# The second attention with its value steps in pairs, eight exponential slots and no staging copies

## The chip, the core and the metric

The kernel runs a four-layer transformer forward pass as one program on one core of a Trainium2 chip. The metric is the device time of one execution in microseconds. Three executions of the kernel before took 3405.69, 3411.26 and 3417.11 us (median 3411.26).

The engines are named as the profile names them: PE is TensorE (matrix multiply; PEld its weight loads), DVE is VectorE, ACT is ScalarE, POOL is GpSimd, SP is SyncE, which here issues DMAs.

## The reference

The input x has 2048 tokens of 128 features. Each layer adds attention(layernorm(x)) and then ffn(layernorm(x)). The change touches only the attention of layer 1, which reads, cut to what matters:

```python
q = jnp.einsum('bsd,dhk->bshk', x, Wq) + bq      # 16 heads of 64
k = jnp.einsum('bsd,dhk->bshk', x, Wk) + bk
v = jnp.einsum('bsd,dhk->bshk', x, Wv) + bv
q = q / jnp.sqrt(jnp.asarray(depth, q.dtype))     # depth = 64
attn = jnp.einsum('bqhd,bkhd->bhqk', q, k)
attn = jax.nn.softmax(attn, axis=-1)
out = jnp.einsum('bhqk,bkhd->bqhd', attn, v)
return jnp.einsum('bqhd,hdm->bqm', out, Wo) + bo
```

The kernel treats the 2048 rows as one sequence: every head forms 2048 x 2048 scores, takes their softmax over the keys, and multiplies by v.

## The kernel before, in words

The program is a row of stages, two per layer. Stage `l1_attention` (lines 639 to 1011) holds the whole change. It works head by head. A head has 16 key tiles of 128 keys, and its queries are four chunks of 512. A **step** is half a key tile: step n = 2 x (key tile) + (half of the queries), so a head has 32 steps, and one counter g = 32 x head + n runs over all 512 steps. Each engine walks the same counter, in an order that is written out by hand (`tasks_of`, and the loops at the ends of the engines' blocks).

In one step PE does this, in this order:
- `scores(2g)`: one score tile of 128 keys x 512 queries in PSUM (`l1a_st`, three banks). It is two matmuls, L830 (high parts, and low part of q against high part of k) and L832 (the rest, and the row maximum as a 65th row). A bank is free again when ACT has read it;
- the first half of the step's list of **aux tasks**, `tasks[:some]`;
- `scores(2g + 1)`;
- in odd steps `values((g - 3) // 2)`: the value product of one key tile, four matmuls L845 that add into `l1a_ov`, each 64 columns wide, two of them side by side in the array;
- the other half of the aux tasks.

ACT turns every score tile into exponentials (L923), in a ring of `PT_SLOTS` = 6 slots, one slot for a step. DVE adds the exponentials of the even steps into `l1a_acc` (`add_rows`, L995), POOL those of the odd steps (L891). A slot is free when its value product and its sum are done.

Aux tasks share a ring of three PSUM banks (`l1a_aux`). PE writes a bank, DVE reads it, and PE may write the bank of aux task k only when DVE has read that of task k - 3. All in one order. The kinds:
- `max`: one 128 x 512 tile of the scores of the **next** head, with queries in rows (PE L795), and its row maximum (DVE L940). There are 64 in a head, spread over steps 0 to 29 (`MAX_STEPS` = 30). After the last DVE makes the negated maxima (L943);
- `mt`, in step 30: PE transposes them (L798), DVE copies them out (L948), and SP places them by DMA as a row of `l1a_QB` (L760). PE waits at L798 for L943, and all that stands behind it on PE waits too;
- `v`, in steps 15 and 17: the value projection of the next head, eight tiles each, 64 columns of output (PE L803, DVE L961);
- `qk`, in steps 16, 18, 20 and 22: the projection to q and k of the head after the next (PE L800). DVE adds the bias, scales q and writes `l1a_full` (L954). When all four are there, in step 24, ACT rounds it to `l1a_hi` (L903), and POOL, behind its sum of step 27, takes `l1a_lo` = full - hi (`cut`, L878). SP copies hi and lo into the operands `QA`, `KA`, `QB`, `KB`;
- `sum`, `sumT`, `out`, in steps 3, 5 and 7, 9, 11, 13: of the head before, the sums over the keys (L808, copied to `l1a_sums`), their transpose and reciprocal, and the output projection (PE L817), which DVE scales and adds to X (L981).

Before the loop stand, in `before`, the projections of heads 0 and 1, the values of head 0, and all 64 maxima of head 0.

## Time and profile before

| what | value |
|---|---|
| median of three executions | 3411.26 us |
| the profiled execution's own time | 3410.64 us |
| its span | 3408.8 us |
| its mean granted TensorE clock | 0.889 |
| PE busy | 3054.8 us, 90% |
| DVE busy | 2357.4 us, 69% |
| ACT busy | 1438.4 us, 42% |
| POOL busy | 800.2 us, 23% |

The stage runs from about 975 to 2562 us of the span. A busy PE counts each matmul from its start to a modelled end, so matmuls in a row overlap, and how fast PE works is read from the starts of successive rows, not from the busy time. Idle time of PE is real idle time. "PEclk" is the clock that was granted to PE, as a share of 2.4 GHz; it has two levels, 1.0 (2.4 GHz) and 0.5 (1.2 GHz).

### The profile page before, as it was taken

The numbers are of one execution on the slowest core, as the hardware profiler recorded it, in microseconds if no ns is written. First come the engines' busy times: TensorE is split into PE (matmuls) and PEld (weight loads), VectorE is DVE, ScalarE is ACT, GpSimd is POOL, SyncE is SP. The second block draws the span as 40 slices with busy tenths as digits, with TensorE's granted clock in tenths as the row PEclk, the third lists the DMA queues.
The fourth block names the chain that finished last, engine by engine and source line by source line (L and its number), as shares of the span: only waits on it lengthen the run. The fifth ranks groups of instructions, "written<-read, shape, count | busy, mean of one in ns | idle before, by whom it ended". The sixth has DMA issues, their size and how long they took to land. (4 is left out here: it accounts for less than half of the span.)

```text
span 3408.8 us, 44140 instructions
## 1 busy us (share of the span) xinstructions
PE 3054.8 (90%) x16200; PEld 1881.8 (55%) x16200; DVE 2357.4 (69%) x4755; ACT 1438.4 (42%) x2539; POOL 800.2 (23%) x621
## 2 busy tenths in 40 slices
PE   5999999999879999999999999999997574666799
PEld 3766666666545555555555555555543242444576
DVE  5788888888247777777777777777735767665553
ACT  3666666666413444444434444444442203001343
POOL 0000000000012444444434444444340000443100
PEclk7999999999778999999999999999998585555798
DMA  3121121110040111111101111111000000000100
GB/s 89 25 47 31 41 48 42 30 43 1 8 112 1 38 38 38 38 38 25 32 19 38 38 38 38 38 25 36 15 1 12 6 2 1 1 1 3 29 1 13
DMA packets 40395, 95.29 MB, mean 28 GB/s; under 512 B 12262, under 2 KB 29340, under 8 KB 30620
## 3 DMA queue, kind: packets, MB, share of 16 engines
q1 hardware_dynamic: 40180, 92.48, 12.2%
q8 instruction: 128, 2.10, 0.3%
q14 instruction: 87, 0.71, 0.1%
HBM read 34.52 MB, written 7.34 MB: 12 GB/s over the span
## 5 line engine op out<-in xcount | busy, mean ns | idle before, releaser
L923 ACT ACTIVATE l1a_PT<-l1a_st 128x512 f32<-128x512 f32 x1024 | 605.7, 598 | 878.5 <-PE l1a_st L832 871.5
L940 DVE TENSOR_REDUCE l1a_m<-l1a_aux 128x1 f32<-128x512 f32 x1024 | 673.4, 686 | 189.2 <-PE l1a_aux L795 173.8
L441 DVE TENSOR_REDUCE l0s_mquad<-l0s_mx 128x1 f32<-128x512 f32 x1024 | 635.5, 684 | 169.5 <-PE l0s_mx L309 169.5
L891 POOL TENSOR_TENSOR l1a_acc<-l1a_acc,l1a_PT 128x1024 f32<-128x1024 f32 x224 | 555.1, 2478 | 717.2 <-ACT l1a_PT L923 717.2
L417 ACT ACTIVATE l0s_PT<-l0s_st 128x512 f32<-128x512 f32 x1024 | 528.7, 602 | 236.8 <-PE l0s_st L325 234.2
L845 PE MATMUL l1a_ov<-l1a_PT,l1a_V 128*64 128x512 f32 x2048 | 512.3, 622 | 0.0
L830 PE MATMUL l1a_st<-l1a_QA,l1a_KA 128*128 128x512 f32 x1024 | 452.1, 442 | 3.2 <-issue 3.1
L325 PE MATMUL l0s_st<-l_QS,l_KS 128*128 128x512 f32 x1024 | 438.1, 431 | 3.7 <-ACT l0s_PT L417 3.6
L309 PE MATMUL l0s_mx<-l_KS,l_QS 120*128 120x512 f32 x1024 | 415.6, 413 | 20.3 <-DMA l_KS<-qk_rows 20.3
L832 PE MATMUL l1a_st<-l1a_QB,l1a_KB 65*128 65x512 f32 x1024 | 414.7, 405 | 0.0
L795 PE MATMUL l1a_aux<-l1a_KA,l1a_QA 128*128 128x512 f32 x1024 | 404.2, 437 | 6.8 <-DMA l1a_QA<-l1a_lo 5.4
L995 DVE TENSOR_TENSOR l1a_acc<-l1a_acc,l1a_PT 128x1024 f32<-128x1024 f32 x224 | 316.9, 1415 | 68.1 <-ACT l1a_PT L923 55.8
L309 PEld LDWEIGHTS l0s_mx<-l_KS,l_QS 120*128 120x128 f32 x1024 | 328.5, 321 | 64.0 <-DMA l_KS<-qk_rows 21.5
L795 PEld LDWEIGHTS l1a_aux<-l1a_KA,l1a_QA 128*128 128x128 f32 x1024 | 200.9, 196 | 177.8 <-DVE l1a_m L940 113.6
L339 PE MATMUL l0s_ov<-l0s_PT,l_V 128*32 128x256 f32 x4096 | 274.1, 385 | 0.0
L845 PEld LDWEIGHTS l1a_ov<-l1a_PT,l1a_V 128*64 128x64 f32 x2048 | 127.7, 140 | 252.5 <-issue 196.1
L325 PEld LDWEIGHTS l0s_st<-l_QS,l_KS 128*128 128x128 f32 x1024 | 195.3, 192 | 114.9 <-ACT l0s_PT L417 87.0
L830 PEld LDWEIGHTS l1a_st<-l1a_QA,l1a_KA 128*128 128x128 f32 x1024 | 197.6, 193 | 97.4 <-issue 54.5
L871 POOL MEMSET l1a_KB<- 1x4096 f32 x1 | 3.5, 3505 | 948.7 <-POOLq L148 948.7
L832 PEld LDWEIGHTS l1a_st<-l1a_QB,l1a_KB 65*128 65x128 f32 x1024 | 197.7, 193 | 50.0 <-issue 13.5
L339 PEld LDWEIGHTS l0s_ov<-l0s_PT,l_V 128*32 128x32 f32 x4096 | 106.8, 109 | 103.7 <-issue 52.4
L981 DVE SCALAR_TENSOR_TENSOR top_X<-l1a_aux,l1a_rinv,top_X 128x128 f32<-128x128 f32 x256 | 72.0, 344 | 52.6 <-PE l1a_aux L817 51.9
(351 smaller groups left out, 3068.6 us busy)
## 6 DMA issues: line engine op xcount, KB each, us to landing
l1a_KA<-l1a_hi SPq DMA_DIRECT2D x32, 512.0 KB, 8.0
l_QS<-qk_rows SPq DMA_DIRECT2D x64, 192.0 KB
l_KS<-qk_rows SPq DMA_DIRECT2D x64, 192.0 KB
l1a_QA<-l1a_hi SPq DMA_DIRECT2D x16, 512.0 KB, 4.6
...
```

The source lines that it names most:

```text
L309: last = nc.tensor.matmul(o, q[:, tile, :], KS[r, h % BUF0, c * CW:(c + 1) * CW], start=True, stop=True)
L325: nc.tensor.matmul(st[:, b % ST0, :], KS[:, h % BUF0, kt * P:(kt + 1) * P], QS[:, h % BUF0, q:q + CW], start=True, stop=True).then_inc(st_ ...
L339: last = nc.tensor.matmul(ov[32 * q:32 * (q + 1), u % 2, :], V[:, u // 2, 2 * n + e, :], PT[:, (2 * r + e) % PT0, q // 2, at], start=(n == ...
L417: nc.scalar.activation(PT[:, g % PT0, b % 2, :], st[:, b % ST0, :], ACT.Exp).then_inc(exp_done, 1)
L441: nc.vector.tensor_reduce(mquad[:, u % 2, tile, g:g + 1], mx[:, n % MX0, :], axis=AX.X, op=ALU.max).then_inc(mx_free[n % MX0], 1)
L795: last = nc.tensor.matmul(o, QA[:, h % 3, q * P:(q + 1) * P], KA[:, h % 3, c * CW:(c + 1) * CW], start=True, stop=True)
L830: nc.tensor.matmul(st[:, u % ST1, :], KA[:, h % 3, kt * P:(kt + 1) * P], QA[:, h % 3, qc * CW:(qc + 1) * CW], start=True, stop=False)
L832: last = nc.tensor.matmul(st[:, u % ST1, :], KB[:, h % 2, kt * P:(kt + 1) * P], QB[:, h % 2, qc * CW:(qc + 1) * CW], start=False, stop=True)
L845: last = nc.tensor.matmul(ov[HD1 * (qc % 2):HD1 * (qc % 2) + HD1, qc // 2, :], V[:, h % 2, kt, :], PT[:, g % PT_SLOTS, (qc % 2) * CW:(qc % ...
L891: nc.gpsimd.tensor_tensor(acc[:, h % 2, 1, :], first, PT[:, g % PT_SLOTS, :], ALU.add).then_inc(added_pool, 1)
L923: nc.scalar.activation(PT[:, g % PT_SLOTS, (u % 2) * CW:(u % 2 + 1) * CW], st[:, u % ST1, :], ACT.Exp).then_inc(exp_done, 1)
L940: nc.vector.tensor_reduce(m4[:, b, q, c:c + 1], src, axis=AX.X, op=ALU.max).then_inc(aux_read, 1)
```

## The change

It touches eight things of the stage:
- `PT_SLOTS` is 8 instead of 6, and values run in every fourth step: in steps 1, 5, 9, ... PE does the value products of two key tiles one behind the other (`g % 4 == 1`). Key tiles 14 and 15 of a head fall into step 1 of the next.
- `MAX_STEPS` is 28 instead of 30, so the 64 maxima are spread over steps 0 to 27, and `mt` stands in step 29.
- The value projection is done for two heads at once, 128 columns of output: one `v` task of four tiles in steps 15 and 17 of every head but the last two (28 instead of 30 tasks in the loop, 8 PE instructions in each instead of 16).
- `full` is gone. ACT makes each quarter of `hi` from PSUM (Identity with bias, L893), in the step of the `qk` task and behind that step's exponentials. DVE then makes that quarter of `lo` from the same bank (scalar_tensor_tensor, L945), and only then is the bank free. POOL's `cut` is gone.
- q is no longer scaled there; the scale stands in the exponential.
- `sums` is gone (it goes into `acc`), and `osb` has one buffer instead of two.
- DVE no longer waits for its own writes before it frees a bank, and the four output rows of a task have one semaphore update.
- Before the loop, `v` has four tasks, and the `lo` of head 1 stands on DVE ahead of all maxima of head 0.

```diff
-PT_SLOTS = 6
+PT_SLOTS = 8
-MAX_STEPS = 30
+MAX_STEPS = 28
...
-                if n == MAX_STEPS:
+                if n == MAX_STEPS + 1:
                     out.append(("mt", h + 1, 0))
-                if n in (15, 17):
-                    out.append(("v", h + 1, (n - 15) // 2))
+                if n in (15, 17) and h + 2 < H1 + h % 2:
+                    out.append(("v", h // 2 + 1, 2 * (h % 2) + (n - 15) // 2))
...
                     elif kind == "v":
-                        for t in range(8):
-                            last = nc.tensor.matmul(o[:, t * HD1:(t + 1) * HD1], xnT[:, (8 * i + t) * P:(8 * i + t + 1) * P],
-                                                    Wv[:, h, :], start=True, stop=True)
+                        for j in range(TPC):
+                            t = TPC * i + j
+                            last = nc.tensor.matmul(o[:, j * P:(j + 1) * P], xnT[:, t * P:(t + 1) * P],
+                                                    Wv[:, 2 * h:2 * h + 2, :], start=True, stop=True)
...
-                    if g % 2 and 3 <= g < H1 * STEPS1 + 3:
-                        values((g - 3) // 2)
+                    if g % 4 == 1 and 5 <= g < H1 * STEPS1 + 5:
+                        values((g - 5) // 2)
+                        values((g - 5) // 2 + 1)
...
-                def cut(h):
-                    pool.wait_ge(hi_done, h + 1)
...
-                    nc.gpsimd.tensor_tensor(lo[:, :], full[:, :], hi[:, :].bitcast(F32), ALU.subtract).then_inc(lo_done, 1)
...
-                        if kt == 13 and h + 2 < H1:
-                            cut(h + 2)
...
-                def round_hi(h):
-                    act.wait_ge(filled, NC * (h + 1))
-                    if h >= 1:
+                def round_hi(h, i):
+                    act.wait_ge(aux_full, slot[("qk", h, i)] + 1)
+                    if h >= 1 and i == 0:
                         act.wait_ge(placed_a[(h - 1) % 3], 64 * ((h - 1) // 3 + 1))
                         act.wait_ge(placed_b[(h - 1) % 2], 32 * ((h - 1) // 2 + 1))
-                    nc.scalar.activation(hi[:, :], full[:, :], ACT.Copy).then_inc(hi_done, 1)
+                    nc.scalar.activation(hi[:, i * CW:(i + 1) * CW], bank(("qk", h, i)), ACT.Identity,
+                                         bias=bias[:, h:h + 1]).then_inc(hi_done, 1)
...
-                    if n == 24 and h + 2 < H1:
-                        round_hi(h + 2)
+                    if n in (16, 18, 20, 22) and h + 2 < H1:
+                        round_hi(h + 2, (n - 16) // 2)
...
                     elif kind == "qk":
-                        if i == 0 and h >= 1:
-                            dve.wait_ge(lo_done, h)
-                        nc.vector.tensor_scalar(full[:, i * CW:(i + 1) * CW], src, bias[:, h:h + 1], factor[:, :],
-                                                ALU.add, ALU.mult).then_inc(filled, 1)
-                        dve.wait_ge(filled, NC * h + i + 1)
-                        dve.sem_inc(aux_read, 1)
+                        at = slice(i * CW, (i + 1) * CW)
+                        dve.wait_ge(hi_done, NC * h + i + 1)
+                        nc.vector.scalar_tensor_tensor(lo[:, at], src, bias[:, h:h + 1], hi[:, at].bitcast(F32),
+                                                       op0=ALU.add, op1=ALU.subtract).then_inc(aux_read, 1)
```

How the orders stand, at three places. First PE from the last two maxima of step 29 in head 5, in the kernel before, to its step 31:

```order
L795 MATMUL l1a_aux<-l1a_KA,l1a_QA 128x512 x2
L830 MATMUL l1a_st<-l1a_QA,l1a_KA 128x512
L832 MATMUL l1a_st<-l1a_QB,l1a_KB 128x512
L845 MATMUL l1a_ov<-l1a_PT,l1a_V 64x512 x4
L795 MATMUL l1a_aux<-l1a_KA,l1a_QA 128x512
L830 MATMUL l1a_st<-l1a_QA,l1a_KA 128x512
L832 MATMUL l1a_st<-l1a_QB,l1a_KB 128x512
L798 MATMUL l1a_aux<-top_ident,l1a_mneg 16x128
L830 MATMUL l1a_st<-l1a_QA,l1a_KA 128x512
L832 MATMUL l1a_st<-l1a_QB,l1a_KB 128x512
L830 MATMUL l1a_st<-l1a_QA,l1a_KA 128x512
L832 MATMUL l1a_st<-l1a_QB,l1a_KB 128x512
```

The maxima (L795) end with the one behind the value block; two matmuls later stands the transpose L798. After the change, on PE, from the second half of step 27 to step 29 of the same head:

```order
L793 MATMUL l1a_aux<-l1a_KA,l1a_QA 128x512
L829 MATMUL l1a_st<-l1a_QA,l1a_KA 128x512
L831 MATMUL l1a_st<-l1a_QB,l1a_KB 128x512
L829 MATMUL l1a_st<-l1a_QA,l1a_KA 128x512
L831 MATMUL l1a_st<-l1a_QB,l1a_KB 128x512
L829 MATMUL l1a_st<-l1a_QA,l1a_KA 128x512
L831 MATMUL l1a_st<-l1a_QB,l1a_KB 128x512
L796 MATMUL l1a_aux<-top_ident,l1a_mneg 16x128
L829 MATMUL l1a_st<-l1a_QA,l1a_KA 128x512
L831 MATMUL l1a_st<-l1a_QB,l1a_KB 128x512
L844 MATMUL l1a_ov<-l1a_PT,l1a_V 64x512 x8
L829 MATMUL l1a_st<-l1a_QA,l1a_KA 128x512
```

Between the last maximum (L793) and the transpose (L796) now stand six score matmuls and no value block; the value block, twice as long (x8), follows the transpose.

Second, PE in steps 18 and 19 of head 5. Before, from the `qk` task on:

```order
L800 MATMUL l1a_aux<-top_xnT,l1a_Wqk 128x512
L830 MATMUL l1a_st<-l1a_QA,l1a_KA 128x512
L832 MATMUL l1a_st<-l1a_QB,l1a_KB 128x512
L795 MATMUL l1a_aux<-l1a_KA,l1a_QA 128x512
L830 MATMUL l1a_st<-l1a_QA,l1a_KA 128x512
L832 MATMUL l1a_st<-l1a_QB,l1a_KB 128x512
L845 MATMUL l1a_ov<-l1a_PT,l1a_V 64x512 x4
L795 MATMUL l1a_aux<-l1a_KA,l1a_QA 128x512
```

After, from the same `qk` task (L798) on:

```order
L798 MATMUL l1a_aux<-top_xnT,l1a_Wqk 128x512
L829 MATMUL l1a_st<-l1a_QA,l1a_KA 128x512
L831 MATMUL l1a_st<-l1a_QB,l1a_KB 128x512
L793 MATMUL l1a_aux<-l1a_KA,l1a_QA 128x512
L829 MATMUL l1a_st<-l1a_QA,l1a_KA 128x512
L831 MATMUL l1a_st<-l1a_QB,l1a_KB 128x512
L793 MATMUL l1a_aux<-l1a_KA,l1a_QA 128x512
L829 MATMUL l1a_st<-l1a_QA,l1a_KA 128x512
L831 MATMUL l1a_st<-l1a_QB,l1a_KB 128x512
L793 MATMUL l1a_aux<-l1a_KA,l1a_QA 128x512 x2
```

The value block that stood behind the `qk` task's second score pair is gone from here, so the next aux tasks follow the `qk` task more closely.

Third, DVE around the same `qk` task. Before:

```order
L940 TENSOR_REDUCE l1a_m<-l1a_aux 128x1 x2
L954 TENSOR_SCALAR l1a_full<-l1a_aux,l1a_bias,l1a_factor 128x512
L995 TENSOR_TENSOR l1a_acc<-l1a_acc,l1a_PT 128x1024
L940 TENSOR_REDUCE l1a_m<-l1a_aux 128x1 x4
```

After:

```order
L933 TENSOR_REDUCE l1a_m<-l1a_aux 128x1 x2
L945 SCALAR_TENSOR_TENSOR l1a_lo<-l1a_aux,l1a_bias,l1a_hi 128x512
L981 TENSOR_TENSOR l1a_acc<-l1a_acc,l1a_PT 128x1024
L933 TENSOR_REDUCE l1a_m<-l1a_aux 128x1 x5
```

L954 was the copy to `full`, which needed only PE; L945 now stands in the same place and needs ACT's quarter of `hi` as well, with the sum L981 (was L995) and the maxima L933 (was L940) behind it.

## Rows read from the trace of the kernel before

**Rows 1.** Waits, 1050 to 2550 us: waiter, releaser, us, times, longest.
```profile
...
ACT l1a_PT L923 <- PE l1a_st L832: 833.3, 688, 4.1
...
PEld l1a_aux L795 <- DVE l1a_m L940: 94.4, 167, 0.8
```

**Rows 2.** Windows, steps 30, 31: length, busy and (count) by engine, PEclk, DMA, GB/s.
```profile
...
1125.49:1135.32 9.83, 6.90 (x19) 2.80 (x17) 4.98 (x7) 2.39 (x4) 6.01 (x3) 0.65 0.27 56
...
1608.98:1617.57 8.59, 5.66 (x19) 2.50 (x17) 4.98 (x7) 2.39 (x4) 5.30 (x3) 0.80 0.31 64
...
2475.63:2480.32 4.69, 4.12 (x19) 1.75 (x17) 2.42 (x4) 2.23 (x4) 1.93 (x2) 1.00 0.01 2
sum 132.35, PE 90.76 PEld 36.22 DVE 72.15 ACT 35.54 POOL 82.74; mean PE 6.05 PEld 2.41 DVE 4.81 ACT 2.37 POOL 5.52
```

**Rows 3.** Timeline, all engines, end of head 5: start, length, engine, line.
```profile
...
1604.78 4.58 POOL L878 TENSOR_TENSOR l1a_lo<-l1a_full,l1a_hi 128x2048 fp32r<-128x2048 f32 x1
...
1606.10 4.34 DVE L995 TENSOR_TENSOR l1a_acc<-l1a_acc,l1a_PT 128x1024 f32<-128x1024 f32 x1
...
1609.21 0.40 PE L832 MATMUL l1a_st<-l1a_QB,l1a_KB 65*128 65x512 f32 x1
...
1610.36 1.87 DVE L940 TENSOR_REDUCE l1a_m<-l1a_aux 128x1 f32<-128x512 f32 x3
1612.27 0.22 DVE L943 TENSOR_REDUCE l1a_mneg<-l1a_m 128x16 f32<-128x64 f32 x1
...
1612.55 0.28 PE L798 MATMUL l1a_aux<-top_ident,l1a_mneg 128*16 128x128 f32 x1 [2.93 <-DVE l1a_mneg L943]
...
1617.57 0.50 PE L830 MATMUL l1a_st<-l1a_QA,l1a_KA 128*128 128x512 f32 x1
```

**Rows 4.** Timeline of PE, one step with a value block.
```profile
...
2007.50 0.40 PE L830 MATMUL l1a_st<-l1a_QA,l1a_KA 128*128 128x512 f32 x1
2007.73 0.40 PE L832 MATMUL l1a_st<-l1a_QB,l1a_KB 65*128 65x512 f32 x1
2008.06 1.94 PE L845 MATMUL l1a_ov<-l1a_PT,l1a_V 128*64 128x512 f32 x8
2009.93 0.50 PE L795 MATMUL l1a_aux<-l1a_KA,l1a_QA 128*128 128x512 f32 x1
2010.26 0.39 PE L830 MATMUL l1a_st<-l1a_QA,l1a_KA 128*128 128x512 f32 x1
```

**Rows 5.** Timeline of PE, two waves of a value block.
```profile
...
2014.07 0.60 PE L845 MATMUL l1a_ov<-l1a_PT,l1a_V 128*64 128x512 f32 x2
...
2014.50 0.60 PE L845 MATMUL l1a_ov<-l1a_PT,l1a_V 128*64 128x512 f32 x2
```

**Rows 6.** Timeline of PE, value projection and output projection.
```profile
...
1567.22 2.00 PE L803 MATMUL l1a_aux<-l1a_Wv,top_xnT 128*128 128x64 f32 x16
1569.03 0.48 PE L830 MATMUL l1a_st<-l1a_QA,l1a_KA 128*128 128x512 f32 x1
...
1548.71 1.16 PE L817 MATMUL l1a_aux<-l1a_Wo,l1a_osb 64*128 64x128 f32 x8
1549.79 0.50 PE L830 MATMUL l1a_st<-l1a_QA,l1a_KA 128*128 128x512 f32 x1
```

**Rows 7.** Groups of VectorE, 1568 to 1600 us.
```profile
...
L995 DVE TENSOR_TENSOR l1a_acc<-l1a_acc,l1a_PT 128x1024 f32<-128x1024 f32 x5 | 6.1, 1223 | 0.9 <-DVE l1a_full L954 0.9
L954 DVE TENSOR_SCALAR l1a_full<-l1a_aux,l1a_bias,l1a_factor 128x512 f32<-128x512 f32 x4 | 3.2, 810 | 0.7 <-PE l1a_aux L800 0.6
```

**Rows 8.** Timeline of VectorE: four output rows.
```profile
...
1543.92 1.13 DVE L981 SCALAR_TENSOR_TENSOR top_X<-l1a_aux,l1a_rinv,top_X 128x128 f32<-128x128 f32 x4 [0.40 <-PE l1a_aux L817]
```

**Rows 9.** Groups of ScalarE, 60 to 330 us.
```profile
...
L376 ACT ACTIVATE l0s_full<-l0s_mx,l0s_bias 128x512 f32<-128x512 f32 x3 | 2.1, 687 | 1.4 <-PE l0s_mx L294 1.4
```

**Rows 10.** Timeline of the start of the attention.
```profile
...
1001.40 38.35 DVE L940 TENSOR_REDUCE l1a_m<-l1a_aux 128x1 f32<-128x512 f32 x64 [4.56 <-PE l1a_aux L795]
...
1005.42 1.91 ACT L903 ACTIVATE l1a_hi<-l1a_full 128x2048 fp32r<-128x2048 f32 x1 [16.98 <-DMA l1a_KB<-l1a_lo]
```

More of the change, by code:

```diff
@@ L716, in tasks_of @@
             return out
-        before = ([("qk", 0, c) for c in range(NC)] + [("v", 0, 0), ("v", 0, 1)] + [("qk", 1, c) for c in range(NC)]
+        before = ([("qk", 0, c) for c in range(NC)] + [("v", 0, c) for c in range(NC)] + [("qk", 1, c) for c in range(NC)]
                   + [("max", 0, i) for i in range(NT * NC)] + [("mt", 0, 0)])
@@ L724, in bank, with read @@
             return aux[:, slot[key] % AUX1, :]
+        def read(key):
+            return slot[key] + 1
         ADDS = NT - 1
@@ L786, in aux_task @@
                     elif kind == "sumT":
-                        pe.wait_ge(sums_out, h + 1)
+                        pe.wait_ge(aux_read, read(("sum", h, 0)))
                     elif kind == "out" and i == 0:
@@ L812, in aux_task @@
                         for j in range(TPC):
-                            last = nc.tensor.transpose(o[:, j * P:(j + 1) * P], sums[:, j * P:(j + 1) * P], ident[:, :])
+                            last = nc.tensor.transpose(o[:, j * P:(j + 1) * P], acc[:, b, 0, j * P:(j + 1) * P], ident[:, :])
                     else:
@@ L816, in aux_task @@
                         for j in range(TPC):
-                            last = nc.tensor.matmul(o[:, j * D:(j + 1) * D], osb[at, b, i // 2, j * P:(j + 1) * P],
+                            last = nc.tensor.matmul(o[:, j * D:(j + 1) * D], osb[at, i // 2, j * P:(j + 1) * P],
                                                     Wo[at, h, :], start=True, stop=True)
@@ L839, in values @@
                     if kt == 0:
-                        pe.wait_ge(v_ready, 2 * (h + 1))
+                        pe.wait_ge(aux_read, read(("v", h // 2, NC - 1)))
                         if h >= 1:
@@ L844, in values @@
                         g = 2 * k + qc // 2
-                        last = nc.tensor.matmul(ov[HD1 * (qc % 2):HD1 * (qc % 2) + HD1, qc // 2, :], V[:, h % 2, kt, :],
+                        last = nc.tensor.matmul(ov[HD1 * (qc % 2):HD1 * (qc % 2) + HD1, qc // 2, :],
+                                                V[:, h // 2 % 2, kt, HD1 * (h % 2):HD1 * (h % 2) + HD1],
                                                 PT[:, g % PT_SLOTS, (qc % 2) * CW:(qc % 2 + 1) * CW],
@@ L887, in _ @@
                         if kt == 1 and h >= 2:
-                            pool.wait_ge(sums_out, h - 1)
+                            pool.wait_ge(aux_read, read(("sum", h - 2, 0)))
                         if kt > 1:
@@ L892, in _ @@
                                                 ).then_inc(added_pool, 1)
-                        if kt == 13 and h + 2 < H1:
-                            cut(h + 2)
             @block.scalar
             def _(act):
-                def round_hi(h):
-                    act.wait_ge(filled, NC * (h + 1))
-                    if h >= 1:
+                def round_hi(h, i):
+                    act.wait_ge(aux_full, slot[("qk", h, i)] + 1)
+                    if h >= 1 and i == 0:
                         act.wait_ge(placed_a[(h - 1) % 3], 64 * ((h - 1) // 3 + 1))
                         act.wait_ge(placed_b[(h - 1) % 2], 32 * ((h - 1) // 2 + 1))
-                    nc.scalar.activation(hi[:, :], full[:, :], ACT.Copy).then_inc(hi_done, 1)
+                    nc.scalar.activation(hi[:, i * CW:(i + 1) * CW], bank(("qk", h, i)), ACT.Identity,
+                                         bias=bias[:, h:h + 1]).then_inc(hi_done, 1)
                 def copy_out(h):
                     act.wait_ge(pv_done, NT * (h + 1))
-                    if h >= 2:
-                        act.wait_ge(aux_full, slot[("out", h - 2, 3)] + 1)
-                    nc.scalar.activation(osb[:, h % 2, :, :], ov[:, :, :], ACT.Copy).then_inc(o_copied, 1)
-                round_hi(0)
-                round_hi(1)
+                    if h >= 1:
+                        act.wait_ge(aux_full, slot[("out", h - 1, 3)] + 1)
+                    nc.scalar.activation(osb[:, :, :], ov[:, :, :], ACT.Copy).then_inc(o_copied, 1)
+                act.wait_ge(w_in, 64)
+                for h in range(2):
+                    for i in range(NC):
+                        round_hi(h, i)
                 for g in range(H1 * STEPS1):
@@ L973, in aux_task @@
                                              src.rearrange("p (j q c) -> p q j c", q=NC, c=32)[:, :, :, 0]
-                                             ).then_inc(rinv_done, 1)
-                        dve.wait_ge(rinv_done, h + 1)
-                        dve.sem_inc(aux_read, 1)
-                    else:
+                                             ).then_inc(aux_read, 1)
+                    else:
+                        dve.wait_ge(aux_read, read(("sumT", h, 0)))
+                        if h:
+                            dve.wait_ge(aux_read, read(("out", h - 1, i)))
+                        else:
+                            dve.wait_ge(bo_added, 1)
                         for j in range(TPC):
                             t = TPC * i + j
-                            dve.wait_ge(x_added, 1 + NT * h - (NT - 1 - t) if h else 1)
-                            nc.vector.scalar_tensor_tensor(X[:, t, :], src[:, j * D:(j + 1) * D], rinv[:, b, t:t + 1],
-                                                           X[:, t, :], op0=ALU.mult, op1=ALU.add).then_inc(x_added, 1)
-                        dve.wait_ge(x_added, 1 + NT * h + TPC * (i + 1))
-                        dve.sem_inc(aux_read, 1)
+                            last = nc.vector.scalar_tensor_tensor(X[:, t, :], src[:, j * D:(j + 1) * D], rinv[:, b, t:t + 1],
+                                                                  X[:, t, :], op0=ALU.mult, op1=ALU.add)
+                        last.then_inc(aux_read, 1)
                 def add_rows(g):
```

62 lines of the change are left out of this document (22 added, 40 removed).

## The prediction

> **What bounds the kernel now.** I read the page first (PE 90% busy, every other engine far below), then the waits of the stretch that holds the heads, then the windows around the end of each head, then PE's timeline, where I read distances between starts.
>
> The waits say that PE leads: ACT waits 833.3 us for score tiles [rows 1], while PE's matmuls are pinned start to start. The one wait of PE for DVE in that view is of its weight loads behind maxima (94.4 us, 167 times, at most 0.8 us), which the running matmuls still cover [rows 1]: so DVE is close behind PE, and this cover is what the change spends.
>
> PE really stops once per head, at its end. In head 5 the last score matmul before the transpose starts at 1609.21, and the transpose L798 at 1612.55 after 2.93 us of idling for L943 [rows 3]. The reason stands on DVE: its sum L995 took 4.34 us, against 1.22 us elsewhere [rows 3, 7], because it started at 1606.10 inside POOL's cut L878 (1604.78, 4.58 us). Behind it came three maxima and L943. The granted clock of this window is 0.80, at others 0.65, where both levels occur (1.2 and 2.4 GHz) [rows 2]; PE had stood 2.9 us before it fell.
>
> A normal single-pass matmul follows its neighbour after 0.23 us (2007.50 to 2007.73). Around a value block it is more: 0.33 into it, 0.33 behind the first matmul after it, and the block takes 1.87 us (2008.06 to 2009.93) [rows 4], of which four waves of two side-by-side matmuls are 4 x 0.43 = 1.72 us (2014.07 to 2014.50) [rows 5].
>
> **The change part by part** (sum against the profiled execution, 3410.6 us, 0.6 us below the median; gains negative).
>
> (a) *Two value blocks back to back.* A block costs 0.10 + 0.10 + (1.87 - 1.72) = 0.35 us beside its streaming [rows 4, 5]. There are 256 key tiles, so 128 blocks fall away: 128 x 0.35 = -45 us. All of it lies on PE's own path. Weight loads inside the joined block are hidden as those between its waves are. Bounds: 0 if each tile of keys pays again, -45 if none does. I take -44, since the trace's waves inside a block also change weights and cost nothing.
>
> (b) *Value projection for two heads.* 16 instructions of 64 columns take 1.81 us (1567.22 to 1569.03). Eight of 128 columns are in the trace as the output projection: 1.08 us (1548.71 to 1549.79) [rows 6]. 30 x 1.81 - 28 x 1.08 = 24, and a little comes back behind it: -23 us. Bounds: 0 (as long as before, if twice the columns took twice as long) and -24.
>
> (c) *The end of a head.* Steps 30 and 31 of heads 0 to 14 take 132.35 us together [rows 2]. Their own work is 8 score matmuls, one block and the small transpose: 8 x 0.234 + 1.72 + 0.35 = 3.94 us, 15 x 3.94 = 59. So 73 us are lost there, 41.6 us of it as idle time (132.35 - 90.76) and the rest at the lower clock. After the change the cut is gone, so L995 takes 1.22 us. But the transpose now comes only six score matmuls (1.4 us) after the last maximum, without a value block in which DVE could catch up, as the order shows. I lay the two out from the end of the block of step 25. PE issues maxima at 0, 0.7, 1.4, 2.1, 2.3 and 3.0 us and arrives at the transpose at 4.7. DVE (a maximum each 0.60, 38.35 us / 64 [rows 10], ready 0.5 us after its matmul starts, the matmul's own 0.40 us [rows 4] and a little) has done three at 2.5, adds until 3.6, does three more until 5.4, then L943 (0.22 us [rows 3]): PE goes on at about 5.9. The wait is 1.2 us, 15 x 1.2 = 18 us, and I expect the clock to hold: 18 - 73 = -55 us. Bounds: -73 (no wait) and 0 (wait and clock as before). The DMA that places the maxima is safe: one score pair, the double block and two steps (some 0.5 + 3.8 + 1.9 us) lie between the transpose and the first score of the next head, where before it was one step and a block (1612.55 to 1617.57 [rows 3]), and PE did not wait.
>
> (d) *The ring of three banks.* This is the price. 64 maxima in 28 steps are 2.29 a step instead of 2.13, and of four steps three and a half now run without a block: PE issues 9 maxima in 5.9 us and then none for 3.8 us, in which DVE can work off only the three that the ring holds. DVE's own load in four steps is 9.1 x 0.60 + 2 x 1.13 = 7.8 us against PE's 9.6, so on average it fits; it is the bunching that stalls. In addition a `qk` bank now waits for ACT: its Identity from PSUM takes 0.69 us [rows 9], then DVE's three-operand instruction, nearest L954 at 0.81 us [rows 7]; it was 0.81 us right after the matmul. Worked out for steps 18 to 21 from the end of a block: PE ends the `qk` matmul at 3.5; ACT's hi is there at 4.3, lo at 5.1, then the sum until 6.2, two maxima until 7.4. PE wants its third bank after `qk` at 5.35 (free, 5.05) and the next at 5.6, which is read only at 6.8: it waits 1.25 us, and another 0.25 us for the second `qk`. In the same way I get 1.25 us for steps 22 to 25, 1.0 us for steps 2 to 5 (the `sum` behind three maxima), 0.7 us and 1.0 us for steps 6 to 13, whose output rows (1.13 us for four, [rows 8]) add as much to DVE as to PE, and 0.3 us for steps 14 to 17. That is 5.75 us per head; 14 heads with `qk` tasks and 3 us for head 14: +84 us. The cover that decides is how far DVE lags when a block begins. Bounds: 1 us per head (+14), and 9 us per head (+126), if DVE takes the 0.69 us of a maximum's own duration instead of 0.60.
>
> (e) *The start.* On DVE the `lo` of head 1 now precedes the 64 maxima of head 0, and the `hi` of head 1 may overwrite only when the DMAs of head 0 have landed. Before, this hi started at 1005.42, released by the last DMA (KB<-lo), while the maxima had begun at 1001.40 [rows 10]. Without the cut these DMAs come some 3 us earlier: 1002.4, and four quarters of hi and lo (about 0.8 us each, and 1 us for the first) put the first maximum at about 1007: +6 us. Bounds: 0 and +10.
>
> (f) *At nothing:* the scale in the exponential (same instruction, ACT has 833 us of waits [rows 1]), eight slots (more room only), one `osb` (free since step 13), the DVE self-waits (0.1 us each, inside (d)), ACT's copying out in step 1, now behind a double block (1.03 us of copy while PE has three score banks free; 15 x 0.5 us if that cover is gone).
>
> Sum: -44 - 23 - 55 + 84 + 6 = -32: **3378 us**.
>
> **Where the skill's rule bears on it.** In the trace the sum that met POOL's cut took 4.34 us instead of 1.22 [rows 3, 7]: it was held as a whole. The Trainium skill, page "SBUF — State Buffer", section "Who interferes with whom", says the port pair that VectorE and GpSimd share is an exclusive lock for whoever starts first. By that rule this trace agrees, and the change, which removes the cut, also brings POOL's sum of an odd step into the time of DVE's sum two steps on, since no block lies between steps 3 and 4 any more: a further delay of up to 1 us in each four steps. It falls mostly into the double block; were it all exposed it would be 1 us x 8 x 15 = 120 us, the third rival by another road.
>
> **The rivals.**
>
> 1. *DVE keeps up.* The stalls of (d) do not come, at most 1 us per head. For it: 7.8 us of DVE work stand against 9.6 us of PE in four steps, and my layout hangs, stall by stall, on tenths. Against: PE's weight loads already wait for DVE 167 times [rows 1]. Time: 3378 - 84 + 14 = 3308.
>
> 2. *The end of the head stays as it is.* DVE is as late at the transpose as before, PE stands about 3 us and the clock falls again: (c) is 0 and the time 3378 + 55 = 3433, slower. It decides from a lag of DVE of four maxima at step 29. Against: the ring holds three, and the 3.1 us of the held sum are gone [rows 3].
>
> 3. *VectorE becomes the pace-setter inside the four steps.* If a maximum costs 0.69 us and each second sum is held for 1 us, DVE needs 9.1 x 0.69 + 2.3 + 1 = 9.6 us for four steps, as much as PE, and each extra (output rows, lo) goes onto the path: 9 us per head, +126 instead of +84: 3420, slower by a little. It decides from 8.3 us of stall per head, (44 + 23 + 55 - 6)/14.
>
> 4. *The joined blocks save nothing*, because the 0.35 us is paid per key tile and not per change of tile width: 3378 + 44 = 3422. Against: the block's inner waves are at 0.43 us [rows 5].
>
> **How the numbers follow.** My forecast 0.54 (its own range 3340 to 3400), DVE keeps up 0.20, head end unchanged 0.06, DVE sets the pace 0.13, joins save nothing 0.07. A measurement of this kernel tells 0.3% (10 us) from no change. Faster than 3401: nine tenths of the first, all of the second and a little of the rest, 0.72. Slower than 3421: half of the third to fifth and some of the first, 0.15. Same: 0.13. The range takes in rival 1 and most of rivals 3 and 4: 3300 to 3422.
>
> **What would show it.** (a) L845 in blocks of 16 with about 3.6 us from first start to the next matmul, not 3.74 or more. (b) eight instructions of the value projection in 1.1 us. (c) the wait L796 for the negated maxima near 1.2 us, 15 times, and a clock of 1.0 in those windows. (d) PE idle before L793 and L798 with DVE as releaser, about 80 us in all, clustered in steps 19, 20, 23 and 24; (e) the first maximum near 1007 us. I am wrong if the idle time of PE before maxima is under 20 us, if L995 is often held above 2 us, or if PE has a wait at the next head's first score.

## The result and the profile after

The changed kernel takes **3376.85 us** (median of four runs, 3368.62 to 3377.22) against 3412.92 us for the kernel before, run beside it: a ratio of 0.9891, 95% interval 0.9868 to 0.9914. The forecast was 3378. The profiled execution took 3376.59 us, 34.1 us less than that of before. Nearly all of this lies in the heads: heads 0 to 14 took 1436.75 us and now take 1397.73 (-39.0), and from the stage's first matmul to its first score it is 70.9 instead of 64.4 us (+6.5).

How one head stands is seen best in windows from the first score of a head to that of the next (length, busy time and count of PE, PEld, DVE, ACT, POOL, granted clock, DMA). Head 5 and the sum of heads 0 to 14, before:

```profile
1521.43:1617.57 96.14, 93.11 (x408) 52.54 (x406) 72.27 (x105) 40.85 (x66) 41.18 (x17) 0.98 0.16 34
...
sum 1436.75, PE 1393.77 PEld 783.08 DVE 1072.74 ACT 609.39 POOL 618.29; mean PE 92.92 PEld 52.21 DVE 71.52 ACT 40.63 POOL 41.22
```

And after:

```profile
1514.01:1608.04 94.03, 89.35 (x391) 50.73 (x390) 67.29 (x106) 40.91 (x70) 38.36 (x15) 1.00 0.16 34
...
sum 1397.73, PE 1329.51 PEld 755.54 DVE 999.62 ACT 609.74 POOL 570.64; mean PE 88.63 PEld 50.37 DVE 66.64 ACT 40.65 POOL 38.04
```

PE has 64 us less to do, but the heads became only 39 us shorter: its idle time in them rose from 43 to 68 us. The waits of the new kernel, same view as [rows 1], name who holds it:

```profile
ACT l1a_PT L916 <- PE l1a_st L831: 790.6, 622, 42.0
...
PEld l1a_aux L793 <- DVE l1a_m L933: 75.7, 120, 1.5
...
DVE l1a_lo L945 <- ACT l1a_hi L893: 54.6, 56, 1.6
...
PE l1a_aux L793 <- DVE l1a_m L933: 36.3, 33, 1.2
...
PE l1a_aux L796 <- DVE l1a_mneg L936: 14.1, 15, 0.9
...
PE l1a_aux L807 <- DVE l1a_m L933: 13.7, 14, 1.0
```

The single stop of a head before, 41.6 us in 15 heads at its transpose, has become 14.1 us there (L796), and 50 us of new waits for DVE's maxima (L793, and L807, the `sum`). These 64 us are nearly all of the 68 that PE is idle. Idle time understates a stop, since the last matmul's modelled tail covers some 0.2 us of each.

The end of head 5, the answer to [rows 3] (start, length, engine, line, then the idle time in brackets):

```profile
1598.38 1.22 DVE L981 TENSOR_TENSOR l1a_acc<-l1a_acc,l1a_PT 128x1024 f32<-128x1024 f32 x1
...
1599.52 1.88 DVE L933 TENSOR_REDUCE l1a_m<-l1a_aux 128x1 f32<-128x512 f32 x3
...
1599.84 2.37 POOL L883 TENSOR_TENSOR l1a_acc<-l1a_acc,l1a_PT 128x1024 f32<-128x1024 f32 x1 [4.20 <-ACT l1a_PT L916]
...
1600.37 0.39 PE L831 MATMUL l1a_st<-l1a_QB,l1a_KB 65*128 65x512 f32 x1
1601.43 0.22 DVE L936 TENSOR_REDUCE l1a_mneg<-l1a_m 128x16 f32<-128x64 f32 x1
1601.56 1.73 DVE L981 TENSOR_TENSOR l1a_acc<-l1a_acc,l1a_PT 128x1024 f32<-128x1024 f32 x1
...
1601.70 0.28 PE L796 MATMUL l1a_aux<-top_ident,l1a_mneg 128*16 128x128 f32 x1 [0.94 <-DVE l1a_mneg L936]
```

A sum of DVE (1598.38) still stands ahead of the last three maxima, but it takes 1.22 us and not 4.34. The maxima are done 1.9 us after they start, and PE waits 0.94 us where it waited 2.93. Steps 28 and 29 of all heads with a transpose, the answer to [rows 2]:

```profile
1599.20:1605.96 6.76, 5.82 (x27) 2.33 (x25) 4.25 (x7) 2.74 (x5) 4.72 (x2) 1.00 0.01 4
...
sum 101.35, PE 87.24 PEld 34.82 DVE 63.68 ACT 40.98 POOL 70.84; mean PE 5.82 PEld 2.32 DVE 4.25 ACT 2.73 POOL 4.72
```

The own work of one such pair of steps is 8 score matmuls and a double block (8 x 0.234 + 3.44 + 0.35 = 5.66 us), so 16.5 us are lost in 15 heads where it was 73, and the clock is at its upper level (PEclk 1.00) in them.

A double block and a value projection, the answers to [rows 4, 6]:

```profile
1566.26 3.65 PE L844 MATMUL l1a_ov<-l1a_PT,l1a_V 128*64 128x512 f32 x16
1569.85 0.50 PE L793 MATMUL l1a_aux<-l1a_KA,l1a_QA 128*128 128x512 f32 x1
1570.18 1.05 PE L802 MATMUL l1a_aux<-l1a_Wv,top_xnT 128*128 128x128 f32 x8
1570.99 0.48 PE L829 MATMUL l1a_st<-l1a_QA,l1a_KA 128*128 128x512 f32 x1
```

16 value matmuls take 3.59 us (1566.26 to 1569.85) and not 2 x 1.87. The projection takes 0.81 us (1570.18 to 1570.99) instead of 1.81.

Where the new waits come from is seen in steps 18 to 20 of head 5, which have no value block between them:

```profile
1573.53 0.69 ACT L893 ACTIVATE l1a_hi<-l1a_aux,l1a_bias 128x512 fp32r<-128x512 f32 x1 [0.27 <-PE l1a_aux L798]
...
1574.32 0.75 DVE L945 SCALAR_TENSOR_TENSOR l1a_lo<-l1a_aux,l1a_bias,l1a_hi 128x512 fp32r<-128x512 f32 x1 [1.05 <-ACT l1a_hi L893]
...
1574.98 1.22 DVE L981 TENSOR_TENSOR l1a_acc<-l1a_acc,l1a_PT 128x1024 f32<-128x1024 f32 x1
...
1575.20 0.42 PE L793 MATMUL l1a_aux<-l1a_KA,l1a_QA 128*128 128x512 f32 x1
1575.37 3.06 POOL L883 TENSOR_TENSOR l1a_acc<-l1a_acc,l1a_PT 128x1024 f32<-128x1024 f32 x1 [5.49 <-ACT l1a_PT L916]
...
1576.12 3.07 DVE L933 TENSOR_REDUCE l1a_m<-l1a_aux 128x1 f32<-128x512 f32 x5
...
1576.86 0.50 PE L793 MATMUL l1a_aux<-l1a_KA,l1a_QA 128*128 128x512 f32 x1 [1.24 <-DVE l1a_m L933]
```

DVE waits 1.05 us for `hi`, makes `lo`, then the sum. The first maximum behind the sum ends at about 1576.8, and only then may PE write the third bank after `qk`: 1.24 us of idling, where the layout in (d) had 1.25. With the tail and the delay of the next `qk` the whole of step 20 takes 3.89 us; undisturbed, in the run with single blocks and half maxima below, it takes 2.08. So 1.8 us are lost in it, where (d) had 1.5.

### The profile page after: what moved, and what is told of

The parts are those of the page before. It is cut to its first block and busy times, and to the rows that moved or that the text cites. A ratio compares the mean times of both kernels' runs of the same rounds, so it can differ in the third digit from the quotient of the medians.

```text
span 3374.8 us, 43476 instructions
## 1 busy us (share of the span) xinstructions
PE 2988.6 (89%) x15944; PEld 1854.7 (55%) x15944; DVE 2293.2 (68%) x4753; ACT 1440.7 (43%) x2587; POOL 748.6 (22%) x605
## 3 DMA queue, kind: packets, MB, share of 16 engines
q8 instruction: 126, 2.06, 0.3%
## 5 line engine op out<-in xcount | busy, mean ns | idle before, releaser
L916 ACT ACTIVATE l1a_PT<-l1a_st 128x512 f32<-128x512 f32 x1024 | 597.5, 598 | 795.4 <-PE l1a_st L831 790.6
L933 DVE TENSOR_REDUCE l1a_m<-l1a_aux 128x1 f32<-128x512 f32 x1024 | 657.7, 682 | 192.1 <-PE l1a_aux L793 191.2
L883 POOL TENSOR_TENSOR l1a_acc<-l1a_acc,l1a_PT 128x1024 f32<-128x1024 f32 x224 | 575.3, 2568 | 742.8 <-ACT l1a_PT L916 742.1
L844 PE MATMUL l1a_ov<-l1a_PT,l1a_V 128*64 128x512 f32 x2048 | 467.7, 598 | 0.0
L793 PE MATMUL l1a_aux<-l1a_KA,l1a_QA 128*128 128x512 f32 x1024 | 416.5, 442 | 41.7 <-DVE l1a_m L933 36.3
L831 PE MATMUL l1a_st<-l1a_QB,l1a_KB 65*128 65x512 f32 x1024 | 407.2, 398 | 0.0
L981 DVE TENSOR_TENSOR l1a_acc<-l1a_acc,l1a_PT 128x1024 f32<-128x1024 f32 x224 | 288.6, 1289 | 96.1 <-ACT l1a_PT L916 96.1
L793 PEld LDWEIGHTS l1a_aux<-l1a_KA,l1a_QA 128*128 128x128 f32 x1024 | 200.0, 195 | 205.6 <-DVE l1a_m L933 95.3
L844 PEld LDWEIGHTS l1a_ov<-l1a_PT,l1a_V 128*64 128x64 f32 x2048 | 135.5, 136 | 266.6 <-issue 252.7
L945 DVE SCALAR_TENSOR_TENSOR l1a_lo<-l1a_aux,l1a_bias,l1a_hi 128x512 fp32r<-128x512 f32 x64 | 47.9, 750 | 80.6 <-ACT l1a_hi L893 80.6
```

What stands on the lines that cost most here:

```text
L793: last = nc.tensor.matmul(o, QA[:, h % 3, q * P:(q + 1) * P], KA[:, h % 3, c * CW:(c + 1) * CW], start=True, stop=True)
L831: last = nc.tensor.matmul(st[:, u % ST1, :], KB[:, h % 2, kt * P:(kt + 1) * P], QB[:, h % 2, qc * CW:(qc + 1) * CW], start=False, stop=True)
L844: last = nc.tensor.matmul(ov[HD1 * (qc % 2):HD1 * (qc % 2) + HD1, qc // 2, :], V[:, h // 2 % 2, kt, HD1 * (h % 2):HD1 * (h % 2) + HD1], PT ...
L883: nc.gpsimd.tensor_tensor(acc[:, h % 2, 1, :], first, PT[:, g % PT_SLOTS, :], ALU.add).then_inc(added_pool, 1)
L916: nc.scalar.activation(PT[:, g % PT_SLOTS, (u % 2) * CW:(u % 2 + 1) * CW], st[:, u % ST1, :], ACT.Exp, scale=1.0 / float(np.sqrt(HD1))).th ...
L933: nc.vector.tensor_reduce(m4[:, q, c:c + 1], src, axis=AX.X, op=ALU.max).then_inc(aux_read, 1)
```

## The experiments

All are edits of the changed kernel, except the third, which is one of the kernel before. Each ratio is to the kernel before on the same chip; its median there was 3408.54 to 3413.69 us, so two times from different chips can differ by some 5 us for nothing. "Head" is the length of one of the heads 1 to 13 in the trace: 96.6 us before (mean), 94.05 after (median; the mean is 94.18, with the one head in which the clock fell).

### One value block in every odd step again, all else as changed

```diff
-                    if g % 4 == 1 and 5 <= g < H1 * STEPS1 + 5:
-                        values((g - 5) // 2)
-                        values((g - 5) // 2 + 1)
+                    if g % 2 and 3 <= g < H1 * STEPS1 + 3:
+                        values((g - 3) // 2)
```

> The changed kernel with one part undone: one value block per odd step again (g - 3), eight slots kept. Theory (price of 0.35 us per block): 128 more blocks, 512 in all halves, +45 us on PE's path; but DVE then gets its pauses more evenly, so some of the 75 us of ring stalls goes back: the time is 3377 + 45 - (0 to 50), I expect 3385. Blocks of 8 take 1.87 us to the next matmul. Rival (joining saves nothing in itself, the gain is elsewhere): blocks of 8 take half of the 3.58 us of a joined one, 1.79, and the time is at or below 3377 - 30.

Measured 3313.22 us, ratio 0.9722 (0.9702 to 0.9742). The expectation was missed by 72 us, and this is the main finding: the pair costs 64 us net. (By the two ratios it is 58 us; by the traces, from the stage's first matmul to its last, 65.) Windows of this kernel:

```profile
1494.10:1583.76 89.66, 89.66 (x392) 50.21 (x390) 67.88 (x105) 40.90 (x69) 38.22 (x16) 1.00 0.17 36
...
sum 1332.19, PE 1332.19 PEld 746.50 DVE 1010.07 ACT 609.91 POOL 569.82; mean PE 88.81 PEld 49.77 DVE 67.34 ACT 40.66 POOL 37.99
```

In heads 0 to 14 PE is never idle, and DVE has as much to do as in the changed kernel (1010 us against 1000). The same steps as above:

```profile
1551.30 0.75 DVE L944 SCALAR_TENSOR_TENSOR l1a_lo<-l1a_aux,l1a_bias,l1a_hi 128x512 fp32r<-128x512 f32 x1 [1.06 <-ACT l1a_hi L892]
...
1551.56 1.94 PE L844 MATMUL l1a_ov<-l1a_PT,l1a_V 128*64 128x512 f32 x8
1551.97 1.22 DVE L980 TENSOR_TENSOR l1a_acc<-l1a_acc,l1a_PT 128x1024 f32<-128x1024 f32 x1
...
1553.10 0.69 DVE L932 TENSOR_REDUCE l1a_m<-l1a_aux 128x1 f32<-128x512 f32 x1
...
1553.43 0.50 PE L793 MATMUL l1a_aux<-l1a_KA,l1a_QA 128*128 128x512 f32 x1
```

DVE waits just as long for `hi` (1.06 us), but its sum now runs under the block. So neither the wait for ACT nor DVE's load is enough by itself to stall PE; it takes the missing block in between.

What a join saves is seen in single steps: step 27 of head 5 with a block (this run) and without (the changed kernel), then step 7 with a block and without (from the two runs with half maxima below, in which PE waits for no maximum in this step):

```profile
1572.09:1575.78 3.69, 3.69 (x17) 1.73 (x15) 3.22 (x5) 1.76 (x3) 1.42 (x1) 1.00 0.45 93
1597.58:1599.20 1.62, 1.62 (x8) 1.32 (x7) 1.61 (x3) 1.19 (x3) 0.00 (x0) 1.00 0.29 56
1485.71:1490.15 4.44, 4.44 (x24) 2.40 (x22) 2.31 (x5) 1.76 (x3) 2.17 (x1) 1.00 0.03 6
1497.94:1500.50 2.56, 2.56 (x15) 1.91 (x14) 2.32 (x5) 1.76 (x3) 0.30 (x1) 1.00 0.03 10
```

A block costs 2.06 us among maxima, but 1.88 us ahead of an output projection (steps 7 and 11), which has to be entered at 0.31 us instead of 0.23 with or without a block ahead of it. In step 31 it is 1.96 us (3.00 and 1.04); step 3, whose undisturbed length no run shows, is put at the same. The second block of a double one costs 1.72 us (3.59 - 1.87). So the eight joins of a head save 4 x 0.34 + 2 x 0.24 + 2 x 0.16 = 2.2 us, not 8 x 0.35 = 2.8. Taken from the 89.6 us of a head here they leave 87.4, and the changed kernel needs 94.05: the pair gains 2.2 us and loses 6.7 us in each head.

### The value projection head by head again

Two tasks of 16 instructions of 64 columns in each head, as before.

> The changed kernel with the value projection per head again (30 tasks of 16 instructions, 64 columns). Theory: the instructions are paid per weight load, so +23 us, 3400. A little of it (up to 8 us) may vanish, as a longer PE task gives DVE time. Rival (cost by columns): no change, 3377.

Measured 3399.29 us, ratio 0.9966 (0.9953 to 0.9978): undoing (b) costs 22 us, as predicted (23). The head is 95.44 us, 1.4 more. The rows above would give 2 x 1.0 us; in the steps it is 2 x 0.9 (15 and 17), and step 16, in which PE's weight loads wait for maxima, gives 0.4 us back.

### The kernel before with a short cut

POOL's `cut` works on 16 columns from head 2 on; the rest of `lo` is left out.

```diff
-                    nc.gpsimd.tensor_tensor(lo[:, :], full[:, :], hi[:, :].bitcast(F32), ALU.subtract).then_inc(lo_done, 1)
+                    at = slice(0, S) if h < 2 else slice(0, 16)
+                    nc.gpsimd.tensor_tensor(lo[:, at], full[:, at], hi[:, at].bitcast(F32), ALU.subtract).then_inc(lo_done, 1)
```

> The kernel before, with POOL's cut for heads 2 to 15 on 16 of 2048 columns (the rest of lo is left out). Nothing else moves. Theory (the held sum causes the wait at the end of a head): L995 there takes 1.22 us, PE's wait at L798 falls from 2.93 us to near 0 (three maxima and L943 are done within the block of step 29 and the score pair), the clock stays at 1.0, and the time falls by 14 x 4.9 = 65 to 70 us, to 3345. Rival (the backlog of maxima makes the wait): PE still waits over 2 us and the time falls by under 15 us.

Measured 3344.11 us, ratio 0.9817 (0.9798 to 0.9836). The transpose waits 0.56 us, and steps 30 and 31 of the 15 heads take 70.30 us, against 132.35 [rows 2]:

```profile
1580.29 0.28 PE L798 MATMUL l1a_aux<-top_ident,l1a_mneg 128*16 128x128 f32 x1 [0.56 <-DVE l1a_mneg L944]
```

```profile
sum 70.30, PE 61.82 PEld 26.21 DVE 36.23 ACT 33.52 POOL 28.85; mean PE 4.12 PEld 1.75 DVE 2.42 ACT 2.23 POOL 1.92
```

None of DVE's 224 sums takes over 1.3 us here. The cut alone, by holding one sum per head, was worth 64 us. The granted clock, still low from the start in the first 5 us of head 0, does not fall again in these heads; in the kernel before it fell in 14 of them.

### Half of each maximum

Every row maximum reads 256 of the 512 columns, once in the changed kernel and once in the one with single blocks.

> The changed kernel with every maximum taken over 256 of the 512 columns (the other half is left out): 0.27 us less DVE work per maximum, PE as it is. Theory (ring stalls behind DVE cost some 75 us in the loop, and the 64 maxima of head 0 run at DVE's pace): stalls nearly vanish, -60 to -75, and the start is faster by 64 x 0.27 = 15 us; the wait at the transpose falls by 0.7 us x 15 = 10: about 3285. Rival (PE has its own pauses that only look like DVE's): -15 us from the start, and no more than -20 besides: 3345.

Measured 3297.58 us, ratio 0.9675 (0.9657 to 0.9692); head 90.23, start to first score 16 us shorter. The start came as expected; in the heads 60 us were won, less than the 70 to 85 expected.

> The kernel with one block per odd step (old start), and every maximum over 256 of the 512 columns (the other half is left out). Theory (with single blocks PE stands at its own floor of 89.6 us a head and no ring stall is left): only the 64 maxima of head 0 gain, about -15 to -17 us, 3297, and heads 1 to 13 stay at 89.6 us. Rival (single blocks still hide stalls behind DVE): heads get shorter by 1 us or more, below 3285.

Measured 3291.09 us, ratio 0.964 (0.9625 to 0.9655). One head of each, pairs first:

```profile
1477.87:1568.11 90.24, 87.79 (x391) 51.24 (x390) 52.65 (x106) 40.91 (x70) 38.98 (x15) 1.00 0.16 36
```

```profile
1467.56:1556.90 89.34, 89.34 (x391) 50.43 (x389) 52.12 (x105) 40.89 (x69) 38.13 (x16) 1.00 0.17 36
```

With single blocks a head changes by 0.3 us only: there PE is at its own work, and 17 of the 22 us lie at the start, where DVE does 64 maxima in a row. The 89.35 us less the 2.2 of the joins, 87.1, are then what a head with pairs takes when nothing stalls. With pairs, a faster DVE wins 3.8 us per head, and 3.1 us over the 87.1 are left, 0.5 in step 3 and 1.3 each in steps 20 and 24: I read these as the part that is not DVE's speed but the order (the turn of a `qk` bank through ACT and DVE is as long as it was).

### The transpose one step later

`MAX_STEPS` = 30 and the transpose in step 30, behind the double block of step 29.

> The changed kernel with the maxima over 30 steps and the transpose in step 30 again; everything else stays. Theory (the wait at the head's end came from the held sum, and the block of step 29 gives DVE time again): no wait at the transpose, but DVE's copy and the DMA of the maxima (1.8 to 2.7 us to landing) now lie ahead of the next head's first score with only 1.4 us of matmuls to cover them: a wait of about 2 us there, and some 1 us per head less of ring stalls. Sum near nothing: 3377, at most 12 us to either side. Rival (the order of the transpose is what the change gained at a head's end): the wait of 3 us and the lower clock come back, +55 us, 3430.

Measured 3371.97 us, ratio 0.9898 (0.9872 to 0.9924); head 93.74, 0.3 us less. No difference that these runs can tell, as expected, but the waits are others than expected: 0.6 us at the transpose (none had been said), 0.8 us at the first score of the next head, for the DMA of the maxima (2 had been said), and for maxima 43 us in all instead of 50. The clock fell three times in the heads instead of once.

### The q/k projection right ahead of the double block

```diff
+QK_AT = (13, 17, 21, 25)
...
-            if h < H1 and h + 2 < H1 and n in (16, 18, 20, 22):
-                out.append(("qk", h + 2, (n - 16) // 2))
+            if h < H1 and h + 2 < H1 and n in QK_AT:
+                out.insert(2, ("qk", h + 2, QK_AT.index(n)))
...
+                    if any(key[0] == "qk" for key in tasks):
+                        aux_task(tasks[some])
+                        some += 1
```

> The changed kernel (value blocks in pairs) with the projections to q and k right ahead of the value block of steps 13, 17, 21 and 25, where PE needs no bank for 3.6 us, instead of behind steps 16, 18, 20 and 22. Theory (half of the ring stalls is a bank that is held while DVE waits for ACT's hi): the stalls of 1.4 us in step 20 and 1.5 us in step 24 go, and PE has a head 2 to 3 us shorter: 14 x 2.5 = -35 us, 3342. Rival (DVE's load between two blocks is what stalls, whatever the bank): the stalls move to other steps and the time stays within 10 us of 3377.

Measured 3345.35 us, ratio 0.9819 (0.9797 to 0.984), 32 us under the changed kernel (expected: 35); head 92.27. The waits of PE for maxima at L794 (the same line) fall from 36.3 to 13.6 us:

```profile
PE l1a_aux L808 <- DVE l1a_m L937: 13.7, 14, 1.0
PE l1a_aux L794 <- DVE l1a_m L937: 13.6, 33, 0.4
```

Step 20 takes 2.32 instead of 3.89 us, of which 0.43 us is the `qk` task's own time. The hold of a `qk` bank is then covered by the block, which shows again that place and not length decides.

**With the `sum` in step 1 as well** (in the double block's step, from step 3):

> The kernel with q and k projected ahead of the blocks, and besides the sum over keys (aux task sum) behind the block of step 1 instead of behind three maxima in step 3. Theory (ring): the 1.1 us stall of step 3 goes, as after a block all three banks are free: 15 x 1.1 = -16 us against the kernel with the q and k projection moved alone. Rival (POOL's sum of step 31 is not done that early): PE waits for it behind step 1 by up to 2 us, and nothing is won.

Measured 3355.8 us, ratio 0.9841 (0.9816 to 0.9866). A miss: it is 10 us slower than without this edit instead of 16 us faster. The head is 91.87 us, only 0.4 less, since what step 3 gives back (2.1 us) turns up in steps 1 and 4 (0.9 and 0.6). And in step 1 of head 15, which has no maxima, the `sum` is alone in its step. By the rule `tasks[:some]` it then comes ahead of the block and waits for POOL's last sum of head 14 (2414.90 + 2.41 = 2417.31), on PE. Behind the last score of head 15 the same happens again:

```profile
2417.42 1.06 PE L808 MATMUL l1a_aux<-l1a_acc,top_ones 128*32 128x512 f32 x8 [1.77 <-issue]
2418.41 0.61 PE L830 MATMUL l1a_st<-l1a_QA,l1a_KA 128*128 128x512 f32 x1
...
2489.23 1.06 PE L808 MATMUL l1a_aux<-l1a_acc,top_ones 128*32 128x512 f32 x8 [3.26 <-issue]
```

PE idles 1.77 and 3.26 us, the clock falls behind each for 3.4 us (from 2418.7 and 2490.3), and from the first score of the last head to the stage's last matmul it is 86.2 instead of 77.9 us. With what the heads before won, the stage is 2.9 us longer than without this edit. The parts behind the stage, which the edit does not touch, are 11 us longer in this profile; why is not shown, so of the 10 us between the medians the edit explains about 3.

### Single blocks and an earlier first maximum

With single blocks, and the four q/k tasks of head 1 between the maxima 16, 24, 32 and 40 of head 0 instead of ahead of them.

> The changed kernel with single value blocks (as in the run with one block per odd step), and at the start the q and k projections of head 1 set between the maxima of head 0 (after maxima 16, 24, 32 and 40) instead of ahead of them. Theory (the start lost some 6 us since DVE stood waiting for hi of head 1, which waited for the DMAs of head 0): the first maximum comes 8 to 9 us earlier, and the four lo's are added to DVE's row of maxima (4 x 0.75 = 3 us): -6 us, 3307. Rival (the maxima of head 0 wait for their own DMAs anyway): no change, 3313.

Measured 3308.63 us, ratio 0.971 (0.9688 to 0.9733). The number fits (3307 had been said), its reason does not: from the stage's first matmul to its first score it is 71.2 us, with the tasks ahead it is 71.0. DVE in this stretch:

```profile
999.59 10.26 DVE L934 TENSOR_REDUCE l1a_m<-l1a_aux 128x1 f32<-128x512 f32 x17 [9.17 <-PE l1a_aux L795]
1011.30 0.75 DVE L946 SCALAR_TENSOR_TENSOR l1a_lo<-l1a_aux,l1a_bias,l1a_hi 128x512 fp32r<-128x512 f32 x1 [1.46 <-ACT l1a_hi L894]
1011.97 4.87 DVE L934 TENSOR_REDUCE l1a_m<-l1a_aux 128x1 f32<-128x512 f32 x8
1018.60 0.75 DVE L946 SCALAR_TENSOR_TENSOR l1a_lo<-l1a_aux,l1a_bias,l1a_hi 128x512 fp32r<-128x512 f32 x1 [1.76 <-ACT l1a_hi L894]
```

The maxima begin at 999.59, but each of the four quarters then costs DVE 1.5 to 1.8 us of waiting, and 0.75 us for `lo`, which is what was won at the front. Against 3313.22 the difference is within the spread of the runs.

### Pairs only where DVE has slack, and fewer slots

The same with key tiles 14 and 15 joined in step 1 of the next head, where step 31 had a block and no maxima stand:

```diff
+                    if g % 2 and 3 <= g < H1 * STEPS1 + 3 and g % STEPS1 != STEPS1 - 1:
+                        if g % STEPS1 == 1:
+                            values((g - 5) // 2)
+                        values((g - 3) // 2)
```

> Single value blocks, the new start, and one pair kept: key tiles 14 and 15 together in step 1 of the next head, where DVE has no maxima behind it. Theory (joining is worth 0.35 us wherever DVE has slack, and costs only where it has none): a head takes 89.25 us instead of 89.60, 16 x 0.35 = -6 us against the kernel without this pair (3308.6): 3303. Rival (the DMA of the maxima, with one block less between the transpose and the next head, is now late): +0.5 to +1 us a head, 3315 to 3320.

Measured **3305.92 us**, ratio 0.9678 (0.9665 to 0.9691), the lowest of the kernels that compute everything: single blocks alone took 3313.22, with the earlier first maximum 3308.63. The head is 89.35 us, without idle time:

```profile
1482.40:1571.75 89.35, 89.35 (x390) 50.31 (x390) 67.72 (x106) 40.87 (x70) 38.25 (x15) 1.00 0.17 36
```

One join per head saves 0.25 us where 0.35 had been said, 15 of them 4 us. The 2.7 us between the medians are within their spread; the head's length is what shows it. The rival, a late DMA of the maxima, did not come.

> Single value blocks, the new start, and six slots for exponentials instead of eight. Theory (the two slots serve only the pairs): no change, 3308.6. Rival (they also give ACT room): ACT waits for slots and a head gets longer by 0.5 us or more, 3317 and up.

Single blocks, the q/k tasks of head 1 among the maxima, and `PT_SLOTS` = 6: 3313.06 us, ratio 0.9705 (0.969 to 0.972), head 89.60 as with eight. With single blocks slots seven and eight gain nothing; whether the pairs need them was not run.

## Why the prediction was right

The total was right to 1 us, the waits stand where they were put, and no rival came out. That the hit is so close is luck: (a) and (b) were 8 and 9 us off in opposite directions, and four runs of this one kernel lie 9 us apart.

- **(a) joined blocks, -44.** The form is right (3.59 us for 16 matmuls, so rival 4 is out), the size is not. The 0.35 us was read at a block among maxima and taken for all; beside the output projections, the `sum` and the next head's start it is 0.16 to 0.24. That makes 2.2 us per head and 36 in all.
- **(b) value projection, -23.** The eight instructions take 0.81 us, not the 1.08 of the output projection [rows 6], so PE's own work fell by 30 x 1.81 - 28 x 0.81 = 32 us. Undoing it cost 22 us, since a third of that gain fell on waits, which are counted in (d).
- **(c) end of a head, -55.** 73 - 16.5 = 56.5 us; the wait is 0.94 us (1.1 with the tail), not 1.2. In heads 0 to 14 the clock fell once (at 1672.3, for 3.4 us) and not 14 times as before. Rival 2 is out. The short cut shows that the held sum, [rows 3], was the cause.
- **(d) the ring of three, +84.** 94.05 - 87.1 - 1.1 = 5.85 us per head where 5.75 stood, 82 us in 14 heads. Step lengths less the undisturbed ones give, for steps 2 to 5, 6 to 9 and so on to 22 to 25: 1.0, 0.5, 0.65, 0.4, 1.8 and 1.5 us, where 1.0, 0.7, 1.0, 0.3, 1.5 and 1.25 had been said (undisturbed lengths from the runs with half maxima). As idle time before maxima only 50 us show, where 80 had been said; the rest is tails and late weight loads. Rival 1 is out: stalls did come. The reason given, bunching, is what the single blocks showed.
- **(e) the start, +6.** Measured 6.5. `hi` of head 1 was released by the DMA and started at 1004.92 (1002.4 had been said), and the maxima of head 0 stood behind its `lo`, from 1010.08. The first `lo` row and the maxima in the profile after:

```profile
1005.71 2.07 DVE L945 SCALAR_TENSOR_TENSOR l1a_lo<-l1a_aux,l1a_bias,l1a_hi 128x512 fp32r<-128x512 f32 x3 [14.25 <-ACT l1a_hi L893]
1009.41 0.75 DVE L945 SCALAR_TENSOR_TENSOR l1a_lo<-l1a_aux,l1a_bias,l1a_hi 128x512 fp32r<-128x512 f32 x1 [1.64 <-ACT l1a_hi L893]
1010.08 38.35 DVE L933 TENSOR_REDUCE l1a_m<-l1a_aux 128x1 f32<-128x512 f32 x64
```

  The first maximum was late by 3 us (1007 had been said), but [rows 10] stood 1.4 us earlier in the program too, and the gap from the last maximum to the first score shrank. That the `lo` ahead of the maxima is the whole reason is not shown: moved among them it won nothing.
- **Rival 3** is out. POOL's sum does hold DVE's, but not where it would cost. The mean of 224 sums is 1289 ns (page of the changed kernel), against 1215 unhindered. 22 of them took over 1.3 us: 15 are the sum right behind the negated maxima of a head (1.73 us, as at 1601.56), when PE has already been let go on, and 7 (2.2 to 2.6 us) stand in head 15, which has no maxima behind them. A maximum does cost 0.60 us in a row, as (d) took it.

```profile
L981 DVE TENSOR_TENSOR l1a_acc<-l1a_acc,l1a_PT 128x1024 f32<-128x1024 f32 x224 | 288.6, 1289 | 96.1 <-ACT l1a_PT L916 96.1
```

What failed was not the forecast but the reading of two of its terms. (a) and (d) were added as a gain and an independent price of the new order, and I did not ask whether (d) is the price of (a). It is: without the pair both go, and by the prediction's own numbers 84 - 44 = 40 us should have come back. The experiment gave 64. The waits at `mt` (16 us) go too, since DVE then has the block of step 27 as cover, and the joins were worth 36 and not 44: 82 + 16 - 36 = 62. The expectation of 3385 for it contradicted the prediction's own (d). So the change as a whole gains by its other parts (no cut: -57, projection: -22), and its headline part loses.

Not tried: joined blocks alone in the kernel before. How the pair would do beside the cut stays open.
